# A gated attention block with a routed feed-forward layer: first expert's weight split, logits copy, second variances and list tables rearranged

## The reference

```python
def _L0_xattn_ref(q, k, v1, mask, W1, b1, W2, b2):   # q: layernorm(x), k = v1 = ctx
    qp = _proj(q, W1, b1, W2, b2)
    kp = _proj(k, W1, b1, W2, b2)
    qk = jnp.einsum('bqd,bkd->bqk', qp, kp) * scale
    qk = qk + mask
    attn = jax.nn.softmax(qk, axis=-1)
    return jnp.einsum('bqk,bkd->bqd', attn, v1)

def _L0_ffn_ref(hidden_states, router_w, router_b, w1, w2):
    ...
    logits = x @ router_w + router_b
    route = jax.nn.softmax(logits, axis=1)
    max_prob = jnp.max(route, axis=1, keepdims=True)
    max_ind = jnp.argmax(route, axis=1)
    for e in range(num_experts):
        h = x @ w1[e]
        a, g = jnp.split(h, 2, axis=1)
        y = jax.nn.silu(a) * g @ w2[e]
        out = jnp.where((max_ind == e)[:, None], y, out)
    out = out * max_prob

x = x + jnp.tanh(g_xattn[0]) * _L0_xattn_ref(_layernorm(x), ctx_1024, ctx_1024, fside, W1, b1, W2, b2)
x = x + jnp.tanh(g_ffn[0]) * _L0_ffn_ref(_layernorm(x), router_w, router_b, w1, w2)
```

## Time and profile before

| what | value |
|---|---|
| median of 3 runs | 452.51 us (451.57 to 454.33) |
| the profiled execution, its own time | 450.66 us |
| its span, from first to last instruction | 448.6 us |
| PE busy | 399.7 us, 89% |
| POOL busy | 246.2 us, 55% |
| DVE busy | 213.7 us, 48% |
| ACT busy | 175.9 us, 39% |
| chain that ended last, by engine | PE 79%, POOL 8%, DVE 6%, DMA 2%, issue 2%, ACT 1% |

### The profile page before, as it was taken

One profiled execution on the slowest core, in us unless ns is written; L12 is line 12 of the kernel. 1 busy time (PEld: TensorE's weight loads), 2 busy tenths in 40 slices (PEclk: granted clock), 3 DMA queues, 4 the chain that ended last, 5 costly groups with the idle time before them and its releaser, 6 DMA issues.

```text
span 448.6 us, 9824 instructions
## 1 busy us (share of the span) xinstructions
PE 399.7 (89%) x2431; PEld 346.0 (77%) x2432; DVE 213.7 (48%) x520; ACT 175.9 (39%) x337; POOL 246.2 (55%) x323
## 2 busy tenths in 40 slices
PE   5998872149999999999999999999999999999990
PEld 4887751037888888888888888888888888888880
DVE  4888995842443443344443444433434434444340
ACT  1276650014543454545532344445433543233230
POOL 2566989020875677887773258728852676232221
PEclk9999996558999999999999999999999999999997
DMA  7951222652333044433342103433331011001010
GB/s 212 361 188 51 97 99 80 102 200 84 119 118 117 23 147 173 145 117 117 123 161 80 36 18 117 135 112 124 117 117 36 4 36 36 24 24 28 24 35 11
DMA packets 29850, 44.27 MB, mean 99 GB/s; under 512 B 8377, under 2 KB 25581, under 8 KB 27791
## 3 DMA queue, kind: packets, MB, share of 16 engines
q1 hardware_dynamic: 24095, 34.58, 23.4%
q0 software_dynamic: 3456, 9.24, 6.3%
q10 hardware_dynamic: 2288, 0.33, 0.5%
HBM read 35.57 MB, written 8.96 MB: 99 GB/s over the span
## 4 chain that ended last, share of the span: by engine, by line
PE 79%; POOL 8%; DVE 6%; DMA 2%; issue 2%; ACT 1%; DVEq 0%; SPq 0%; POOLq 0%; ACTq 0%
PE py L1093 22%; PE pa L1075 22%; PE pg L1075 21%; PE ph L1085 7%; POOL w_lo L411 2%; PE px L1060 2%; POOL rstd L395 2%; PE ps_s L1004 1%; DMA ctx_in<-in_ctx 1%; POOL slot_iota L432 1%; PE ps_p L948 1%; DMA x_sorted<-residual_rows,idx_gather 1%; DVE x_all L728 1%; PE ps_xt L920 1%; POOL mask_c L387 1%
## 5 line engine op out<-in xcount | busy, mean ns | idle before, releaser
L875 DVE TENSOR_TENSOR ht_lo<-ph,ht_hi 128x512 fp32r<-128x512 f32 x70 | 48.4, 692 | 135.9 <-ACT ht_hi L610 135.9
L481 POOL TENSOR_TENSOR w_lo<-staging,w_hi x84 | 107.4, 1307 | 6.7 <-ACT w_hi L631 4.0
L610 ACT CAST ht_hi<-ph 128x512 fp32r<-128x512 f32 x70 | 41.1, 587 | 121.3 <-PE ph L1085 86.0
L1093 PE MATMUL py<-w_hi,ht_hi 128*128 x280 | 81.3, 290 | 0.8 <-DVE out_tile L883 0.8
L1093 PE MATMUL py<-w_hi,ht_lo 128*128 x280 | 78.4, 280 | 0.0
L1093 PE MATMUL py<-w_lo,ht_hi 128*128 x280 | 78.3, 280 | 0.0
L470 POOL DMA_INDIRECT out<-out_tile,idx_now x34 | 34.7, 1019 | 72.0 <-DVE out_tile L883 71.3
L1075 PE MATMUL pa<-w_hi,xt_hi 128*128 (+1 forms) x140 | 58.8, 420 | 0.8 <-ACT xt_hi L592 0.8
L439 POOL DMA_INDIRECT x_sorted<-residual_rows,idx_now x34 | 35.6, 1048 | 40.8 <-DVE x_norm L858 22.7
L1075 PE MATMUL pg<-w_hi,xt_hi 128*128 (+1 forms) x140 | 56.1, 401 | 0.0
L1075 PE MATMUL pa<-w_lo,xt_hi 128*128 (+1 forms) x140 | 56.1, 401 | 0.0
(11 more groups left out here) (167 smaller groups left out, 577.5 us busy)
## 6 DMA issues: line engine op xcount, KB each, us to landing
staging<-in_L_ffn_w SPq DMA_DIRECT2D x24, 1024.0 KB, 4.9
residual_rows<-x_all SPq DMA_DIRECT2D x8, 532.0 KB, 3.6
x_all<-in_x SPq DMA_DIRECT2D x8, 512.0 KB, 9.9
x_sorted<-residual_rows,idx_now POOLq DMA_INDIRECT x34, 3.9
out<-out_tile,idx_now POOLq DMA_INDIRECT x34, 2.5
w_in<-in_L_xattn_W SPq DMA_DIRECT2D x2, 256.0 KB, 4.7
ctx_in<-in_ctx SPq DMA_DIRECT2D x1, 308.0 KB
mask_in<-in_fside_1xSxS ACTq DMA_DIRECT2D x1, 308.0 KB, 11.2
```

The source lines that it names most:

```text
L481: lo = nc.gpsimd.tensor_tensor(out=w_lo[:, bass.ds(dst + q * QW, QW)], in0=staging[:, bass.ds(src + q * QW, QW)], in1=w_hi[:, bass.ds(dst ...
L610: nc.scalar.copy(ht_hi[:, j], ph[j][:]).then_inc(hhi_ready[j], 1)
L875: nc.vector.tensor_tensor(out=ht_lo[:, j], in0=ph[j][:], in1=ht_hi[:, j].bitcast(FP32), op=ALU.subtract).then_inc(hlo_ready[j], 1)
L1093: last = mm(py[:, 0:D], ht[:, j, c * P:(c + 1) * P], w[:, bass.ds(slot + (DC * PW + (j * HC + c) * D), D)], start=j == 0 and n == 0, stop= ...
```

## The change

Five things are changed.

1. *Weights.* ACT casts all six chunks behind its part of the attention loop instead of one in each of the steps 0 to 5. POOL subtracts chunk 0 in step 7 and chunk 1 in step 8, chunks 2 and 3 behind the loop, and 4 and 5 behind the first gather, instead of one in each of the steps 1 to 6. PE's first up product waits for two pieces (DC = 2), not three; the third belongs to the down product, which waits for it by itself (L1126).
2. *Logits.* ACT copies them out of PSUM in front of its softmax, instead of DVE.
3. *Variances.* For groups 0 to 5 DVE makes no bn_aggr; POOL joins the even and odd halves of the statistics by eight small operations. Groups 6 and 7 are as before. DVE's statistics of a group now wait for norm2 of the group two before.
4. *List tables.* slot_iota and col_iota hold one group of 4 tokens and are read again for each group; slot_hot and col_hot are laid out by group, in three rounds of 3, 3 and 2 groups (12, 12 and 8 tiles of tokens).
5. *Waits.* FIRST is 4, and DVE no longer waits for the last stores (rows_stored) ahead of the tables; SP still does, ahead of the gates.

```diff
-    HT = NT // 2
-    FIRST = 3
+    ROUNDS = ((0, 3), (3, 6), (6, NG))
+    FIRST = 4
+    JOINED = NG - 2
...
-        slot_iota = sb1("slot_iota", [P, P, NT], FP16)
-        col_iota = sb1("col_iota", [P, COLS, NT], FP16)
-        slot_hot = sb1("slot_hot", [P, P, NT], FP16)
-        col_hot = sb1("col_hot", [P, COLS, NT], FP16)
+        slot_hot = sb1("slot_hot", [P, NG, P, B], FP16)
+        col_hot = sb1("col_hot", [P, NG, COLS, B], FP16)
+        slot_iota = sb1("slot_iota", [P, P, B], FP16)
+        col_iota = sb1("col_iota", [P, COLS, B], FP16)
...
             def norm2(g):
                 r = g % 2
                 pool.wait_ge(mv2_ready, g + 1)
-                link(nc.gpsimd.tensor_scalar(var_eps2[:, r], mv2[:, r, :, 1], EPS, None, ALU.add))
+                if g < JOINED:
+                    even, odd = bn2[:, r, :, 0:3], bn2[:, r, :, 3:6]
+                    nc.gpsimd.tensor_tensor(out=parts2[:, 0], in0=even[:, :, 1], in1=odd[:, :, 1], op=ALU.subtract)
+                    nc.gpsimd.tensor_tensor(out=parts2[:, 1], in0=even[:, :, 2], in1=odd[:, :, 2], op=ALU.add)
+                    link(nc.gpsimd.tensor_tensor(out=parts2[:, 2], in0=even[:, :, 1], in1=odd[:, :, 1], op=ALU.add))
+                    nc.gpsimd.tensor_scalar(mv2[:, r, :, 0], parts2[:, 2], 0.5, None, ALU.mult)
+                    nc.gpsimd.tensor_scalar(parts2[:, 4], parts2[:, 1], 1.0 / D, EPS, ALU.mult, ALU.add)
+                    link(nc.gpsimd.tensor_tensor(out=parts2[:, 3], in0=parts2[:, 0], in1=parts2[:, 0], op=ALU.mult))
+                    link(nc.gpsimd.tensor_scalar(parts2[:, 5], parts2[:, 3], 0.25, None, ALU.mult))
+                    link(nc.gpsimd.tensor_tensor(out=var_eps2[:, r], in0=parts2[:, 5], in1=parts2[:, 4], op=ALU.add))
+                else:
+                    link(nc.gpsimd.tensor_scalar(var_eps2[:, r], mv2[:, r, :, 1], EPS, None, ALU.add))
...
-                if 0 <= i - 1 < N_CHUNK:
-                    low0(i - 1)
+                if 0 <= i - (NG - 1) < 2:
+                    low0(i - (NG - 1))
                 if i == NG - 1:
                     pool.wait_ge(first_stored, 16 * FIRST)
...
+            for c in range(2, 2 * DC):
+                low0(c)
...
                 gather_rows(t, idx_gather[:, t:t + 1])
+                if t == 0:
+                    for c in range(2 * DC, N_CHUNK):
+                        low0(c)
...
+            def copy_logits(g):
+                act.wait_ge(masked_ready, g + 1)
+                scored = ps_s[g % 2][:, 0:B * KW].rearrange("p (b k) -> p b k", b=B)
+                nc.scalar.copy(x_all[:, g, :, D:XW], scored[:, :, KEYS:KW]).then_inc(x_logits_ready, 1)
...
                 if i < NG:
+                    copy_logits(i)
                     softmax(i)
-                if i < N_CHUNK:
-                    high0(i)
+            for c in range(N_CHUNK):
+                high0(c)
...
-                nc.vector.tensor_copy(x_all[:, g, :, D:XW], scored[:, :, KEYS:KW]).then_inc(x_logits_ready, 1)
...
                 dve.wait_ge(x1_ready, B * (g + 1))
+                if 2 <= g < JOINED + 2:
+                    dve.wait_ge(rstd2_ready, g - 1)
                 for b in range(B):
                     last = nc.vector.bn_stats(bn2[:, r, b], x_all[:, g, b, 0:D])
...
-            dve.wait_ge(rows_stored, 16 * (NG - FIRST))
...
+                def of_group(table, m):
+                    return table[:].unsqueeze(1).to_broadcast([P, n, m, B])
+
+                def of_token(v, m):
+                    return v.rearrange("p (g b) -> p g b", b=B)[:, at].unsqueeze(2).to_broadcast([P, n, m, B])
...
-            pe.wait_ge(w_ready, PIECES)
+            pe.wait_ge(w_ready, DC)
```

More of the change, by code:

```diff
@@ L111, in flamingo_block @@
         rstd2 = sb1("rstd2", [P, NG, B])
+        parts2 = sb1("parts2", [P, 6, B])
         var_eps1 = sb1("var_eps1", [P, NG, B])
@@ L734, in stats2 @@
                 dve.wait_ge(x1_ready, B * (g + 1))
+                if 2 <= g < JOINED + 2:
+                    dve.wait_ge(rstd2_ready, g - 1)
                 for b in range(B):
                     last = nc.vector.bn_stats(bn2[:, r, b], x_all[:, g, b, 0:D])
[L737 to L743, removed]
+                if g < JOINED:
+                    last.then_inc(mv2_ready, 1)
+                else:
+                    last.then_inc(bn2_ready, 1)
+                    dve.wait_ge(bn2_ready, g - JOINED + 1)
+                    for b in range(B):
+                        last = nc.vector.bn_aggr(mv2[:, r, b], bn2[:, r, b])
+                    last.then_inc(mv2_ready, 1)
             for i in range(NG + 2):
@@ L815, in _ @@
             dve.wait_ge(first_stored, 16 * FIRST)
[L816 to L823 removed]
+            for first_group, end_group in ROUNDS:
+                at = slice(first_group, end_group)
+                n = end_group - first_group
+                def of_group(table, m):
+                    return table[:].unsqueeze(1).to_broadcast([P, n, m, B])
+                def of_token(v, m):
+                    return v.rearrange("p (g b) -> p g b", b=B)[:, at].unsqueeze(2).to_broadcast([P, n, m, B])
+                nc.vector.tensor_tensor(out=slot_hot[:, at], in0=of_group(slot_iota, P), in1=of_token(pos_f[:, 1], P),
                                         op=ALU.is_equal)
[L825 removed]
+                link(nc.vector.tensor_tensor(out=col_hot[:, at], in0=of_group(col_iota, COLS),
                                              in1=of_token(pos_f[:, 0], COLS), op=ALU.is_equal))
[L827 removed]
+                nc.vector.tensor_tensor(out=col_hot[:, at], in0=col_hot[:, at], in1=of_token(token_v[:], COLS),
                                         op=ALU.mult).then_inc(hot_ready, 1)
@@ L1046, in _ @@
             mm(ps_xt[0][:, 0:E * NT], not_before[:], hot, start=True, stop=True).then_inc(ranks_psum, 1)
-            for t in range(NT):
-                if t % HT == 0:
-                    pe.wait_ge(hot_ready, t // HT + 1)
-                last = mm(ps_s[0][:, 0:COLS], slot_hot[:, :, t], col_hot[:, :, t], start=t == 0, stop=t == NT - 1)
+            for r, (first_group, end_group) in enumerate(ROUNDS):
+                pe.wait_ge(hot_ready, r + 1)
+                for g in range(first_group, end_group):
+                    for b in range(B):
+                        last = mm(ps_s[0][:, 0:COLS], slot_hot[:, g, :, b], col_hot[:, g, :, b],
+                                  start=g == 0 and b == 0, stop=g == NG - 1 and b == B - 1)
             last.then_inc(lists_step, 1)
```

12 lines of the change are left out of this document (3 added, 9 removed).

## The result

The changed kernel takes 471.07 us (median of 6 runs, 467.83 to 472.06) against 452.04 for the one before (by now the median of 6 runs too): a ratio of 1.039, 95% interval 1.0353 to 1.0426, slower by 19 us. The forecast was 453.5, in a range of 449.4 to 456.4. The profiled execution took 468.53 us with a span of 466.5, 17.9 more than before. Two places hold it: the first up product starts 4.8 us later (105.06 against 100.26), and the expert loop, whose code the change doesn't touch, takes 13 us longer.

The account below looks back on a forecast made before the run. PE bounds the expert loop, so only the time before it, with its waits on POOL, could change. Routing +1.45 and list tables -0.45 gave +1.0 us: median 452.5 becomes 453.5, range 449.4 to 456.4.

Parts of the forecast that it names:

- which the change doesn't touch: Loop over expert tiles, PE busy from 200 to 300 us: a gain can only come before the first expert matmul.
- Or the expert loop itself longer than before: Last of the listed signs that the forecast is wrong, on the loop over expert tiles; no size or chance given.
- x_norm is held: Rival behind the first gather: a low half takes the port before x_norm, +3.05 in all, 455.6 us; chance 0.27.
- Attention loop: Loop ahead of routing: 4.8 us per group instead of 5.28, group 5's statistics at 63.3, 3.1 us earlier.
- POOL after the loop: POOL's norms, two low halves and small iotas before routing: routing starts at 77.1 against 79.39, -2.3 us.
- Routing beside two low halves: DVE's routing: work_b and work_a held by POOL's low halves, work_a ends at 82.2 against 80.73; -2.3 becomes +1.45.
- List tables: Tables and matmuls before the gather: three rounds +0.35, fewer last matmuls -1.0, restarts +0.2; together -0.45 us.
- half speed: Rival on the list tables: short runs of 4 tokens cost 4 us more, 457.5 us; chance 0.05.
- Gather and x_norm: Behind the first gather: x_norm goes in between two low halves at no cost; if held, +2.05 us.

Follow-up runs that it names:

- e2: Changed kernel with 2 already-met wait instructions added at the start of DVE's program, its loop at 302 instead of 300; 456.29 us, 1.0112 of before.
- e10: Changed kernel with 128 more already-met wait instructions at the start of DVE's program, its loop at 428; 477.6 us, 1.0547 of before.
- e8: Kernel before with only the weights change (part 1), DVE's loop at 330; 461.44 us, 1.0217 of before.
- e7: Kernel before with only the list tables and the dropped wait (parts 4 and 5), DVE's loop at 332; 451.14 us, 0.9962 of before.
- e6: Changed kernel with DVE's loop at 302 and the fifth and sixth low halves behind the second gather, not the first; 453.88 us, 1.0048.

## Why the prediction was wrong

**The step that failed** is the sentence on the expert loop, "which the change doesn't touch", from which every number followed as front time alone. The instructions are the same, but the change takes 30 instructions off DVE's program ahead of the loop, and with that x_norm comes 0.08 us later in its tile. Before it started 2.33 us behind the subtractions, 0.2 us before the second's end, and was let in there. I had that start in the earlier trace rows (153.41 against 151.34, 2.07 behind; others are at 2.33) and used it for routing, not for asking how near the loop stood to an edge. From 2.40 on it waits for the third, in 12 tiles, and the loop takes 13 us more. Undone alone (e2) it gives back 12 to 15 of the 18 to 19 us, and e10 makes it again. "Or the expert loop itself longer than before" stood among the signs of error, without a price or a chance.

**The rest, 4 us, is the front.** Without the loop's part the time is 456.3, at the upper end of my range (456.4) and near the rival "x_norm is held", 455.6, but that is in part luck: x_norm was not held itself, it stood behind tab_k, which cost 3.4 us and not 2.05, and POOL's chain was off by another +1.1, the tables by -0.6.

*Attention loop.* Right in the main. Periods of 4.7 to 5.0, forecast 4.8, with DVE's own operations back to back and 0.2 us of waiting for PE. Group 5's statistics end at 63.13, forecast 63.3, but half a microsecond of it is the earlier first masked of this execution; counted from there they come 2.8 us earlier instead of 3.1. That parts 2 and 3 bring nothing in it (e8 against the changed kernel) the forecast didn't ask.

*POOL after the loop.* Too short by 1.1: best at 78.16, forecast 77.1. The two iotas take 1.22 + 0.59 us, not 0.85 together: an eighth of the numbers costs three tenths of the time. A joined norm2 takes 3.96 us, not 3.73. Counted from the first masked, best is 0.7 us earlier, where 2.3 were forecast.

*Routing beside two low halves.* Right, and it was the term that decided the front's sign. From best's start to work_a's end 5.02 us, forecast 5.1, where before it was 1.34. Best, with one source, ran at 0.42 beside the same low half. The Trainium skill, "SBUF — State Buffer", section "SBUF: two separate sides", gives the lock to a DVE operation with two SBUF inputs against a GpSimd operation that reads SBUF; with work_b at 2.09 the trace agrees.

*List tables.* Better than forecast: from slot_hot to past_hole 5.75 us against 6.76, -1.0 instead of -0.45. The rounds of 12 cost DVE 1.82 us as forecast. The mis-sized term is PE's: the last 8 matmuls take 0.60 us where 16 took 1.96, 0.07 us each instead of 0.12, at a granted clock of 0.50, the lower level, in both. Shape and type are the same, and what differs is the layout of the tables, in which the numbers that one matmul reads stand 4 and not 32 apart; e7 has 0.61 for 8, e8 with the old tables 1.96 for 16. e7 shows a small gain of tables and small iotas together, most of it from the iotas; half speed is out (0.96 us for 1536 elements).

*Gather and x_norm.* Wrong. I asked whether x_norm gets in between two low halves. It never came to that: DVE still had small operations to do behind the gather's issue, and one of them, a tab_k, reads two columns from SBUF. It was held from 96.76 to 102.34 over both low halves, without a gap between them, and x_norm, ACT's cast and the first product stood behind it: +2.6 for x_norm against the earlier trace rows and +0.8 through ACT. e6 removed it and got 2.4 us back. That tab_k began 0.9 us before the first low half's shown start is seen in e8 too; why it was held from there, and not let in between the two, as x_norm is in the expert loop, stays open.

In sum, against before: -1.23 for best, +3.68 held in routing, -1.01 for the tables, +2.60 and +0.77 behind tab_k: +4.8, as the first product shows, and 13 for the loop. From the first masked on it is -0.70 for best and +5.3 in all.

## What to carry to other kernels

A steady loop that runs beside another engine can stand 0.1 us from an edge: before touching the program ahead of it, look at where its held operation starts within the other engine's instruction, and after each change compare the loop's period first. When it moved without cause, a few empty instructions ahead of the loop tell at once whether its place is to blame. Work that is put on GpSimd "behind the critical path" must be checked against every DVE operation with two SBUF inputs that is still due, the one-element ones too.

## What was not expected of the hardware

- The first DVE operation behind the loop's branch starts 0.68 instead of 0.60 us behind the operation ahead of it when the loop begins at instruction 300 or 428 of DVE's program, and not at 301, 302, 330 (changed kernel), 330, 332 or 364 (kernel before). Two places 128 apart suggest a period of 128 instructions; more places were not tried, and why a place is bad is not shown; the runs show only that the branch starts 0.10 us later at these two places and that the jump back takes 0.1 us more at 300, 301, 302 and 428. The Trainium skill, "Runtime: NRT & Kernel Launch", section "Instruction fetch mechanics", speaks of a program that is streamed in blocks of 256 instructions and of a stall where a branch leaves the window; a period of 256 alone does not fit, since 300 and 428 are both bad. Nor is it a fetch in each tile: no packed trace has an instruction packet behind 150 us, and the slow tiles of the changed kernel lie between 169 and 390 us.
- x_norm gets in between two subtractions of 1.27 us on POOL when it starts 2.33 us behind the first one's start, and waits for the next when it starts at 2.40 to 2.43 (12 of 12 in the changed kernel and in e10; up to 2.36 none in e2).
- A 128x1 operation was held for 5.58 us, 35 times its own length, in each of the seven traces that have two low halves right behind the first gather.
- The same fp16 matmuls of 55 columns took 0.12 us each when their numbers stood 32 apart and 0.07 when they stood 4 apart, both at a granted clock of 0.50.
